# Function tables of ScalarE loaded by evaluations of a column of zeros, and one instruction less in the layer norm's root, in a four-layer transformer kernel

## The reference, cut to what matters

```python
def _layernorm(x, axis=-1, eps=1e-05):
    m = jnp.mean(x, axis=axis, keepdims=True)
    v = jnp.var(x, axis=axis, keepdims=True)
    return (x - m) / jnp.sqrt(v + eps)

# in each of the four layers (l = 0 to 3)
xn = _layernorm(x, axis=-1)
x = x + attention_l(xn, ...) + ffn_l(xn, ...)
```

## Time and profile before

| | |
|---|---|
| median of 3 runs | 1496.31 us (1495.48 to 1500.05) |
| profiled execution, its own time | 1495.88 us |
| its span, first to last instruction | 1493.8 us (2.1 us lie around it) |
| TensorE busy | 1393.0 us, 93% of the span |
| mean granted TensorE clock | 0.968 of full speed |

### The profile page before, as it was taken

The page is one execution under the profiler, slowest core; times in us unless marked ns, Lnnn a source line. Parts: engine busy times, 40 slices in busy tenths (PEclk is TensorE's granted clock), DMA queues, the critical chain, the costliest instruction groups (busy, mean ns, idle before and its releaser), DMA issues.

```text
span 1493.8 us, 25842 instructions
## 1 busy us (share of the span) xinstructions
PE 1393.0 (93%) x9284; PEld 1208.4 (81%) x9284; DVE 1001.5 (67%) x1828; ACT 714.6 (48%) x1860; POOL 460.6 (31%) x358
## 2 busy tenths in 40 slices
PE   5899999899999796989999999999999999848998
PEld 5778887577777575779999999999999999737887
DVE  5676666589998645466666766667666776764554
ACT  5666666522221222246555665556565566422332
POOL 5211111123221732415343443525243444124000
PEclk9899999999999896899999999999999999969999
DMA  5010001132230001011112021201102120010000
GB/s 183 1 45 1 2 2 43 43 107 85 88 116 0 22 1 52 29 36 41 60 29 70 28 70 28 70 8 35 56 28 70 28 70 28 1 63 8 15 14 28
DMA packets 31237, 63.71 MB, mean 43 GB/s; under 512 B 4684, under 2 KB 5351, under 8 KB 31170
## 3 DMA queue, kind: packets, MB, share of 16 engines
q1 hardware_dynamic: 29938, 61.89, 12.9%
q10 hardware_dynamic: 1232, 0.93, 0.2%
HBM read 60.68 MB, written 2.13 MB: 42 GB/s over the span
## 4 chain that ended last, share of the span: by engine, by line
PE 88%; DVE 7%; ACT 2%; issue 2%; DMA 1%; POOL 0%; DVEq 0%; POOLq 0%; SPq 0%; ACTq 0%
PE PS L356 21%; PE PS L358 20%; PE PS L357 20%; PE PS L1670 3%; PE PS L1980 3%; PE PS L1967 2%; PE PS L1965 2%; PE PS L1966 2%; PE PS L1603 2%; PE PS L1690 2%; PE PS L1651 1%; PE PS L1623 1%; PE PS L1686 1%; PE PS L1956 1%; PE PS L1532 1%
## 5 line engine op out<-in xcount | busy, mean ns | idle before, releaser
L356 PE MATMUL PS<-XNH,E_WL 128*128 128x256 f32 x768 | 215.4, 280 | 0.8 <-DVEq L351 0.8
L358 PE MATMUL PS<-XNH,E_WH 128*128 128x256 f32 x768 | 215.2, 280 | 0.0
L357 PE MATMUL PS<-XNL,E_WH 128*128 128x256 f32 x768 | 214.6, 279 | 0.0
L557 POOL TENSOR_TENSOR E_sw<-E_sw,rope2s 128x1024 f32<-128x1024 f32 x64 | 104.8, 1638 | 274.8 <-ACT E_sw L609 274.8
L1365 DVE TENSOR_REDUCE E_nb<-PS 128x4 f32<-128x512 f32 x64 | 61.3, 958 | 177.4 <-PE PS L1967 177.4
L609 ACT ACTIVATE E_sw<-PS 64x256 f32<-64x256 f32 (+1 forms) x128 | 89.5, 699 | 121.0 <-PE PS L358 119.5
L356 PEld LDWEIGHTS PS<-XNH,E_WL 128*128 128x128 f32 x768 | 144.8, 189 | 2.5 <-DVEq L351 1.2
L357 PEld LDWEIGHTS PS<-XNL,E_WH 128*128 128x128 f32 x768 | 144.8, 189 | 1.3
L358 PEld LDWEIGHTS PS<-XNH,E_WH 128*128 128x128 f32 x768 | 144.5, 188 | 0.0
L466 POOL TENSOR_TENSOR E_WL<-raw,E_WH 128x512 fp32r<-128x512 f32 x80 | 109.9, 1403 | 106.7 <-ACT E_WH L609 106.2
L825 ACT ACTIVATE E_p<-PS,E_nb 128x128 f32<-128x128 f32 (+1 forms) x256 | 104.2, 419 | 33.0 <-DVE E_nb L1365 33.0
(11 more groups left out here) (294 smaller groups left out, 3991.1 us busy)
## 6 DMA issues: line engine op xcount, KB each, us to landing
raw<-in_w SPq DMA_DIRECT2D x97, 256.0 KB, 2.8
words<-in_words SPq DMA_DIRECT2D x11, 768.0 KB, 4.1
wo<-in_wo SPq DMA_DIRECT2D x32, 256.0 KB, 3.7
zb<-z_scratch SPq DMA_DIRECT2D x11, 384.0 KB, 4.9
scb<-in_scales SPq DMA_DIRECT2D x11, 384.0 KB, 5.5
X<-in_x SPq DMA_DIRECT2D x8, 256.0 KB, 5.8
out<-X SPq DMA_DIRECT2D x8, 256.0 KB, 2.1
wo<-in_w SPq DMA_DIRECT2D x4, 256.0 KB, 5.2
```

The lines of the kernel that those rows point to most:

```text
L356: nc.tensor.matmul(o, sl, mh, start=first, stop=False, **shared)
L357: nc.tensor.matmul(o, sh, ml, start=False, stop=False, **shared)
L358: return nc.tensor.matmul(o, sh, mh, start=False, stop=last, **shared)
L557: nc.gpsimd.tensor_tensor(E_sw[:, heads, :], E_sw[:, heads, :], rope2s[:, :].unsqueeze(1).broadcast_to([P, heads.stop - heads.start, SEQ]) ...
```

## The change

**The tables.** A new tile `table` of 128 x 1 is zeroed by GpSimd at the start of the program, ahead of its other fills, and `load_table(f)` evaluates f on it in place, which makes the table load stand there. Nine such evaluations are added: the root's table at the very start, and then, each ahead of the barrier that ends a stage, at the end of layer 0's feed-forward, of layer 1 and of layer 2's attention; the exponent's right after the second root of layer 0, and after the roots of layers 2 and 3; the sigmoid's at the end of layer 0's attention and after the root of layer 1. In layers 1 and 2 the evaluation after the root stands behind the four copies of `dense_heads`. There are nine table loads then, and none at another place.

**The root.** `var` now holds 0.25 (v + 1e-5), made by the same instruction, so that `sd` is half the root. The refined value is then sd + var/sd without the factor 0.5, and L948 (L998 in layer 0) goes.

```diff
-        LN_SIGNALS = dict(stat=TT, aggr=TT, var=1, sd=1, c=5, xn=TT, tp=TT, hi=TT, lo=TT)
-        LN0_SIGNALS = dict(LN_SIGNALS, var=2, sd=2, c=10)
+        LN_SIGNALS = dict(stat=TT, aggr=TT, var=1, sd=1, c=4, xn=TT, tp=TT, hi=TT, lo=TT)
+        LN0_SIGNALS = dict(LN_SIGNALS, var=2, sd=2, c=8)
...
+            nc.gpsimd.memset(table[:, :], 0.0).then_inc(a["table"], 1)
             nc.gpsimd.memset(STK[:, :, 3 * D0:S0], 0.0).then_inc(a["init"], 1)
...
+            def load_table(function):
+
+                nc.scalar.activation(table[:, :], table[:, :], function)
+
-            def normalise(l, XT=None, each=None, first=None):
+            def normalise(l, XT=None, each=None, first=None, later=None):
 
                 ln_wait(act, l, "var", 1)
                 nc.scalar.activation(LN[l]["sd"][:, :], LN[l]["var"][:, :], ACT.Sqrt).then_inc(ln["sd"], 1)
                 if first is not None:
                     first()
+                load_table(later)
...
             ready = [prepared(-1, g) for g in FIRST]
+            act.wait_ge(a["table"], 1)
+            load_table(ACT.Sqrt)
             split0((0,))
             roots(0, slice(0, 2))
...
             roots(1, slice(2, TT))
+            load_table(ACT.Exp)
             scale_rows(2)
...
             take_inverses(NB * G0)
+            load_table(ACT.Sigmoid)
             finish(act, 2)
...
             ffn_gate(NF - 1, 0)
+            load_table(ACT.Sqrt)
             finish(act, 3)
...
-            normalise(1, XT1, first=lambda: dense_heads(U_W1, W1H))
+            normalise(1, XT1, first=lambda: dense_heads(U_W1, W1H), later=ACT.Sigmoid)
...
+            load_table(ACT.Sqrt)
             finish(act, 4)
...
+            load_table(ACT.Sqrt)
             finish(act, 6)
...
-            normalise(3, each=l3_heads)
+            normalise(3, each=l3_heads, later=ACT.Exp)
...
-                V.tensor_scalar(B["var"][:, :], B["mv"][:, :, 1], 1e-5, None, ALU.add).then_inc(ln["var"], 1)
+                V.tensor_scalar(B["var"][:, :], B["mv"][:, :, 1], 1e-5, 0.25, ALU.add, ALU.mult).then_inc(ln["var"], 1)
...
                 V.tensor_tensor(B["tmp"][:, :], B["tmp"][:, :], B["sd"][:, :], ALU.add).then_inc(ln["c"], 1)
                 ln_wait(dve, l, "c", 3)
-                V.tensor_scalar(B["tmp"][:, :], B["tmp"][:, :], 0.5, None, ALU.mult).then_inc(ln["c"], 1)
+                V.reciprocal(B["rstd"][:, :], B["tmp"][:, :]).then_inc(ln["c"], 1)
                 ln_wait(dve, l, "c", 4)
-                V.reciprocal(B["rstd"][:, :], B["tmp"][:, :]).then_inc(ln["c"], 1)
-                ln_wait(dve, l, "c", 5)
```

More of the change, by code:

```diff
@@ L81, in build_program @@
         stats = keep("stats", [P, TT, 6])
+        table = keep("table", [P, 1])
         XNB, TB = 4, 3
@@ L794, in l2_heads @@
                     head(n % RAW, g * (U_L2_G // RAW) + (n // RAW + 1), E_WH[:, u, :])
-            normalise(2, XT2, lambda tt: l2_heads(0, range(tt - 2, tt - 1)) if tt >= 2 else None, lambda: dense_heads(U_WB2, W2H))
+            normalise(2, XT2, lambda tt: l2_heads(0, range(tt - 2, tt - 1)) if tt >= 2 else None, lambda: dense_heads(U_WB2, W2H), later=ACT.Exp)
             act.wait_ge(d2["g_ps"], 1)
```

14 lines of the change are left out of this document (6 added, 8 removed).

## The result

| | before | after |
|---|---|---|
| median of 20 runs each | 1496.82 us | 1494.35 us |
| ratio of the two | | 0.998, 95% interval 0.9971 to 0.9989 |
| profiled execution, its own time | 1495.88 us | 1492.31 us |
| its span | 1493.8 us | 1490.3 us |

The changed kernel is faster by 0.2%, some 3 us. The forecast was 6.4 us, 1489.9 us, with a range up to 1493.8, so both the size and the range missed. A later comparison on one chip with other kernels gave 1492.77 us for the changed kernel against 1496.7, ratio 0.9977 (0.9963 to 0.9991).

What follows compares the result with a forecast made beforehand. TensorE, busy 93% of the span, was taken as the bound, with time won only where it stands still. Terms -0.70 + 0.13 - 2.06 - 2.48 - 1.28 = -6.4 gave 1489.9 us, range 1486.0 to 1493.8.

Steps and rivals of the forecast that it cites:

- What bounds the kernel: Whole kernel: TensorE, busy for 93% of the span; time can be won only where it stands still for ScalarE's chain.
- The root's instruction: Heads of layers 1 and 2: without L948 one GpSimd rest less is met, -1.23 and -1.20 us.
- The load ahead of the root: Heads of layers 1 and 2: the load between `var` and `sd` moves under idle time, -1.28 us each.
- The fourth W1L: Layer 1's dense start: the products wait for GpSimd's fourth rest, so layer 1 gains 2.06 us, not 2.51.
- Layer 2's head: Layer 2, up to the first products needing XT: no weight's rest is waited for, 1.28 + 1.20, -2.48 us.
- Loads behind `dense_heads`: Layer 1: the sigmoid's load and evaluation end as the first XT copy's input is ready, costing 0 to 0.02 us.
- Layer 0, start: Program start: root sooner, but two-input column steps blocked by GpSimd's rests; only its 0.77 us pause closes up, -0.70 us.
- Layer 0, second part: Between layer 0's second root and ScalarE's scaled rows: the exponent's load now stands there, +0.13 us.
- Layer 3 and recall: Layer 3: products still wait for a DMA, 0; recall: the load lies inside TensorE's idle time, -1.28 us.
- the rival of dearer switching: Layers 0, 1 and 2: a load followed by waiting work costs its length once more, 1493.3 us; chance 0.05.
- The clock: Layers 1, 2 and recall: each clock rise assumed to move with the work ahead; a missing recall fall wins up to 1.6.
- the rival of the unmoved rises: Layers 1 and 2: clock rises stay put, so the gains halve to 1.03 + 1.24, 1492.2 us; chance 0.14.

Runs made afterwards that it cites:

- the root alone: Kernel before with 0.25 in `var` and L948 and L998 out, no new tile, table loads where they were: 1494.08 us, ratio 0.9984.
- tables alone: Changed kernel with L948 and L998 back, later tiles 64 bytes further than in the kernel before: 1492.16 us, ratio 0.9976.
- the kernel without a new tile: Changed kernel with `table` put into an unused column of shift_k, so no other tile moves: 1489.18 us, ratio 0.9948.

## Why the prediction was wrong

Point by point, in the order of the prediction:

- **What bounds the kernel**: half right. The forecast steps did lie where TensorE waited. That "time can be won only where TensorE stands still" is what failed; the point on what no term covered tells how.
- **The root's instruction**: right in kind and size. 1.23 and 1.20 were forecast; the root alone measured 1.22 and 1.21. The reading of L948 as a wait that ends with GpSimd's instruction is borne out: the same wait is met once less. That the two wait for access to SBUF is argued, no run separates it from another cause. The Trainium skill (SBUF — State Buffer, Who interferes with whom) has such a shared pair of ports, taken whole by one of the two engines, with two SBUF inputs as one of the forms that meet it; the rows of layer 0's start (0.73 and 1.24 us, both with two inputs) agree.
- **The load ahead of the root**: right, 1.28 each (tables alone).
- **The fourth W1L**: right. Layer 1 won 2.05 at its dense start against 2.06, and 2.50 at its first transpose.
- **Layer 2's head**: 2.47 against 2.48.
- **Loads behind `dense_heads`**: right. The evaluation ended at 497.39, and the copy began at 497.30, the two overlapping by their usual 0.1.
- **Layer 0, start**: 1.06 against 0.70. The two-input steps were blocked, as assumed. Of the difference, 0.30 us is the first rest's start (6.43 in place of 6.73), that is when the first weights landed; in other kernels with the same code ahead of it the first transpose was anywhere from 9.7 to 11.0 us (10.62 here, and 9.89 in the second trace of the same kernel, where the variance sat through the first rest and both two-input steps took 0.16). The term had no bound for that, and its nearness is luck.
- **Layer 0, second part**: +0.14 against +0.13 (root to first scaled row 1.62 us in place of 1.48).
- **Layer 3 and recall**: right, 0 and -1.28, with the 2.61 and 0.67 us of the rows above in place of 2.6 and 0.7.
- **The pause behind a table load**: not there. The next instruction begins 0.01 us behind the load (495.90 + 1.28 = 497.18, then 497.19), at all nine loads of this trace, so the rival of dearer switching falls, and the 1.38 us of the Trainium skill (ScalarE: Activation LUTs, What ACT_TABLE_LOAD costs) isn't seen here.
- **The clock**: half right. I had assumed that each rise moves with the work ahead of it. Granted clock in after, where the dense products of layer 1 and 2 begin, and behind recall's idle time:

```profile
499.50:505.40 5.90, 5.80 (x16) 4.27 (x15) 4.30 (x5) 1.31 (x3) 5.90 (x6) 0.50 0.15 47
...
505.40:506.40 1.00, 1.00 (x11) 1.00 (x10) 0.00 (x0) 0.00 (x0) 1.00 (x2) 0.97 0.00 0
...
594.79:597.55 2.76, 2.76 (x8) 2.18 (x9) 0.48 (x1) 0.28 (x1) 1.27 (x1) 0.50 0.34 105
1370.02:1374.00 3.98, 3.66 (x29) 3.46 (x30) 1.87 (x7) 1.84 (x5) 0.00 (x0) 1.00 0.00 0
```

  In layer 1 the dense start came 4.6 us sooner and the rise only some 1.7 (505.4 in place of 507.1), so that twelve products ran at 1.2 GHz where six had: it gave back 1.3 of the 4.6 us. This is the rival of the unmoved rises, at one of its two places. In layer 2 the rise came 8.5 us sooner (597.6 in place of 606.1) for a start 6.3 us sooner, and won 1.0 back. At recall the fall at 1374.1 didn't come, and some 0.8 was won. Together the three won 0.5 us, so that the clock hardly shows in the sum, which is luck. A low stretch lost was one of the prediction's own signs of being wrong.
- **What no term covered, and where the prediction failed**: the first step, "time can be won only where TensorE stands still", which put everything outside those places at nothing. Of the new tile it counted only the fill by GpSimd, at 0, and never its 32 bytes. TensorE was taken as a fixed quantity in layer 2's loop, and there, where it never stands still, the changed kernel lost 4.84 us of its lead, by a spacing of 119.8 ns in place of 116.5 to 117.9. With the new tile out of the way, the same change gives 1489.18 us against a forecast of 1489.9, and its ratio's interval is 0.9929 to 0.9966, in which the forecast's 0.9957 lies.
- Against that, 1.5 us were won between layer 0's first transpose and layer 1's variance, where the sum had +0.13. Some 0.7 of it was won ahead of the feed-forward, where the spacing of the products with WQH and WQL allows 1.1 (some 480 products by 2.3 ns), and 0.7 in the feed-forward, whose products with XNH and XNL against FWH got closer, by 2.3 us summed over their spacing. The chain of waits of the feed-forward shows why so little came of the 2.3 us: TensorE's products make 90% of it before and in the kernel without a new tile, and 51% in after, with VectorE's steps on the weights (F_q, F_t, FWL) and sums (F_acc) for most of the rest. By this reading VectorE sets the pace there once the products are closer, and this is the 11% on the page; no run tried a faster VectorE.
- **Sums of the text**: two falls of the clock are 2 x 4.56 = 9.1 us and not 9.3, so that rival stood at 1499.0. Nothing else hangs on it.

**What stays open.** Why the distance of XNH and XNL to E_WH and E_WL sets the spacing, and its pattern: from 80096 to 80224 bytes in steps of 32 it gave 117.3, 119.8, 118.4, 115.8 and 118.2 ns on average, and no rule of the five follows. The two slowest places seen have one thing in common: 80128 bytes in layer 2 (119.8 ns) and 98432 - 32896 = 65536 in layer 0 (119.2 ns) are both multiples of 256, and 32 bytes further it was 118.4 and 116.9. Two cases are no rule, and no run was made for it. The Trainium skill (TensorE: Matmul & The Clock Gate, Step-by-step: what each phase is for) has two independent read ports for the streamed and the loaded operand, and says that loading the next weights "doesn't steal SBUF read bandwidth from the running matmul"; here the spacing of one kind of product changes by up to 4 ns in 120 with where its two operands lie to each other, which that sentence doesn't lead one to expect; whether the reads are what gets slower isn't shown. The Trainium skill (SBUF — State Buffer, Who interferes with whom) says of PE and ACT that they "never wait on anyone"; the runs don't show whether TensorE waits for another engine or for itself. Also open is the 1.2 us by which one kernel's loop was shorter at equal addresses, and the products of PH with VL, whose spacing changed at an unchanged distance.

## What to carry to other kernels

A new tile, even one column, moves every tile that is allocated after it. In a kernel that TensorE bounds, that can cost or bring more than the edit it was made for: set the k-th matmul of both traces side by side, and where a lead melts evenly at full clock with no waits, compare the spacing of one kind of matmul and then the addresses. Put small helpers into unused bytes of an existing tile (or at the end of the allocation, which wasn't tried here), and try the distance between the streamed and the loaded operand of the commonest product in steps of 32 bytes, since the spacing came out the same, to a few tenths of a ns, in both traces of the two programs that were traced twice, and was worth 9 us in the loop between the worst and the best of five. Short steps of VectorE beside GpSimd are priced by how many of GpSimd's instructions the chain meets, not by their own length: one step less was worth 1.21 us, and its own length is 0.17.

## What the runs showed of the hardware that was not expected

- The spacing of 128x256 products by the distance of their operands: 115.6 to 119.8 ns at full granted clock. Two programs were traced twice, and each gave the same stretch of 4089 matmuls within 0.05 us (584.13 and 584.14, 575.20 and 575.15).
- At the slowest distance the products of five of the six units stood 120.0 ns apart. At the best one they stood 113.4 apart in some units and 117.7 in the others, and from one projection of the six units to the next the two sets changed places. The second trace of the same program has them the other way round from the fifth projection on: the same products at the same addresses at one rate in one trace and at the other in the next, while the sum over the loop is the same. Why isn't known. Before, the spacing ran through a series such as 113, 116, 118, 120.
- The clock's rise keeps no fixed distance from the start of dense work: 2.4 us before and 5.3 after in layer 1, with the same matmuls in the same order.
- A column of VectorE with one SBUF input, the variance of layer 0, took 1.27 us in place of 0.17 when it began 0.01 us behind an instruction of GpSimd (1.17 to 1.27 in eight traces), while each reciprocal under a running one took 0.17 to 0.20.
